# Switch experts' constants and first weights loaded in cross attention's projection; gather, both normalisations and transposes before retention in one block

## What is computed

```python
x = _layernorm(x + cross_attention(x, ctx))          # res @ Wproj + bproj at its end
# switch experts
logits = x @ Wr + br;  probs = softmax(logits)
gate = max(probs);  idx = argmax(probs);  mask = one_hot(idx, E)
pos = (cumsum(mask) * mask);  mask = mask * (pos < C)      # C = 100 slots of an expert
expert_in = einsum('nd,nec->ecd', x, dispatch)             # rows of x, times their gate
h  = relu(einsum('ecd,edf->ecf', expert_in, W1) + b1)
eo = einsum('ecf,efd->ecd', h, W2) + b2
x  = _layernorm(x + einsum('ecd,nec->nd', eo, combine))
# retention
xn = _ln(x, norm1_w, norm1_b)                              # a second normalisation of the same rows
q, k, v = xn @ wq + bq, xn @ wk + bk, xn @ wv + bv
...
x  = x + (silu(xn @ wg + bg) * groupnorm(retain(q, k, v))) @ wo + bo
```

## Time and profile before

| | us |
|---|---|
| median of 3 runs | 2859.72 |
| lowest, highest | 2859.01, 2860.47 |
| profiled execution, device time | 2862.07 |
| its span, from the first to the last instruction | 2860.3 |
| mean granted clock of TensorE, share of full speed | 0.938 |
| busy: TensorE, VectorE, ScalarE, GpSimd | 2507.9, 1402.8, 897.6, 557.9 |

### The profile page before, as it was taken

One profiled execution on the slowest core, in us unless ns is written; L12 is line 12 of the kernel. 1 busy time (PEld: TensorE's weight loads), 2 busy tenths in 40 slices (PEclk: granted clock), 3 DMA queues, 4 the chain that ended last, 5 costly groups with the idle time before them and its releaser, 6 DMA issues. The chain is left out here.

```text
span 2860.3 us, 32983 instructions
## 1 busy us (share of the span) xinstructions
PE 2507.9 (88%) x12313; PEld 1264.8 (44%) x12313; DVE 1402.8 (49%) x2005; ACT 897.6 (31%) x1869; POOL 557.9 (20%) x485
## 2 busy tenths in 40 slices
PE   7899999988999999896499899885997669999994
PEld 4544444434455555534245454353664323333331
DVE  5788888721578886721425512285444521111113
ACT  3644544402533334401112210085333112212210
POOL 0055555500000000001201100000000033343343
PEclk9899999999999999998799899997998879999997
DMA  2022222136535544308340000112000151560633
GB/s 86 25 72 82 75 85 79 66 87 241 187 112 185 175 139 120 126 15 243 117 156 0 2 39 3 50 41 88 1 1 1 53 233 52 232 265 23 261 101 116
DMA packets 94553, 288.64 MB, mean 101 GB/s; under 512 B 26924, under 2 KB 57288, under 8 KB 80188
## 3 DMA queue, kind: packets, MB, share of 16 engines
q1 hardware_dynamic: 59308, 158.34, 16.8%
q0 software_dynamic: 35104, 128.36, 12.6%
HBM read 449.40 MB, written 47.11 MB: 174 GB/s over the span
## 5 line engine op out<-in xcount | busy, mean ns | idle before, releaser
L684 POOL TENSOR_TENSOR x_rows<-ms_state,mb_C_everywhere 128x800 f32<-128x800 f32 x128 | 241.2, 1884 | 312.5 <-DVE ms_state L661 181.4
L694 PE MATMUL psum<-ms_context,mb_key_w 128*128 128x361 f32 x768 | 269.4, 487 | 23.0 <-ACT x_rows L604 9.6
L915 PE MATMUL psum<-at_Wv,at_context 128*128 128x512 f32 (+1 forms) x576 | 266.1, 601 | 0.0
L661 DVE TENSOR_TENSOR_SCAN ms_state<-ms_decay,psum 128x800 f32<-128x800 f32 x128 | 232.2, 1814 | 58.2 <-ACT ms_decay L611 41.3
L2639 PE MATMUL psum<-tf_W,tf_x_T 128*64 128x512 f32 x1024 | 232.3, 601 | 8.9 <-DMA tf_W<-in_L_W,tt_weight_row 8.9
L2661 PE MATMUL psum<-tf_W,tt_hidden 128*64 128x512 f32 x1024 | 227.2, 595 | 0.2 <-DMA tf_W<-in_L_W,tt_weight_row 0.2
L2694 ACT ACTIVATE tt_hidden<-psum,tf_b 128x64 f32<-128x64 f32 x512 | 111.7, 329 | 364.7 <-PE psum L2650 364.7
L694 PEld LDWEIGHTS psum<-ms_context,mb_key_w 128*128 128x128 f32 x768 | 136.3, 190 | 163.0 <-ACT x_rows L599 64.4
L2584 POOL DMA_INDIRECT tf_W<-in_L_W,tt_weight_row x128 | 126.9, 991 | 231.9 <-PE psum L2639 151.9
L1016 ACT ACTIVATE at_prob<-psum,at_neg_max 100x722 f32<-100x722 f32 x128 | 110.4, 863 | 145.9 <-DVE at_neg_max L1078 145.6
L1078 DVE TENSOR_REDUCE at_neg_max<-psum 100x1 f32<-100x722 f32 x128 | 115.6, 904 | 78.3 <-PE psum L936 77.9
(11 more groups left out here) (459 smaller groups left out, 3870.5 us busy)
## 6 DMA issues: line engine op xcount, KB each, us to landing
at_piece<-in_L_W_f POOLq DMA_DIRECT2D x24, 1024.0 KB, 6.3
keys_dram<-x_rows SPq DMA_DIRECT2D x128, 180.5 KB, 1.9
at_k_cols<-keys_dram SPq DMA_DIRECT2D x64, 361.0 KB, 3.2
sf_W<-in_L_W SPq DMA_DIRECT2D x16, 1024.0 KB, 7.5
tf_W<-in_L_W SPq DMA_DIRECT2D x8, 2048.0 KB, 26.0
ms_context<-in_ctxT SPq DMA_DIRECT2D x16, 541.5 KB, 4.4
at_context<-in_ctxT SPq DMA_DIRECT2D x8, 1083.0 KB, 5.1
ternary_dram<-at_piece_made POOLq DMA_DIRECT2D x14, 512.0 KB, 4.0
```

What stands on the lines that cost most here:

```text
L661: nc.vector.tensor_tensor_scan(state[:, n % RH, :], decay[:, g % RA, :, :].rearrange("p b l -> p (b l)"), drive[:, n % RD, :], 0.0, ALU.mu ...
L684: nc.gpsimd.tensor_tensor(seen[:, n % RH, :], state[:, n % RH, :], cC[:, n, :], ALU.mult).then_inc(weighed, 1)
L694: last = nc.tensor.matmul(side[:, 0:SH], lhsT=wk[:, k, e * P:(e + 1) * P], rhs=keys[:, h, k, :], start=(k == 0), stop=(k == KC - 1))
L915: last = nc.tensor.matmul(bank[0:rows_of(t), :], lhsT=ctxT[:, b % 2, k, t * P:t * P + rows_of(t)], rhs=wv[:, k, h * BANK:(h + 1) * BANK], ...
```

## The change

1. `project_norm` gets `early`, called on SP after the projection's own loads, and `keep`, by which SP stores each normalised sequence of x to DRAM as soon as it is ready, in 8 transfers of 200 KB. `switch_experts` now allocates its tiles first and passes in, as `early`, the loads of Wr and the five constants, of W1 and W2 of experts 0 and 1, and of b1 and b2. The loop of weight loads has one turn less. The release between the two blocks is gone.
2. The logits are made with x^T as stationary operand (100 columns) and Wr (8 columns) streaming, 4 matmuls a sequence, directly in the layout that was made by transposes; ScalarE's copies and the transposes are gone.
3. `gather_norm` and `normed_cols` in front of retention become one block, `gather_cols`. The second normalisation follows from the first's statistics: with v the variance, its rows are (x - mean) * (v (1 + eps) + eps^2)^-0.5. VectorE makes these, from the unscaled sum, and they are transposed. The rows of `c.x`, normalised once, are made by GpSimd, 8 `tensor_scalar` of 100x512, after VectorE's, and the block ends after them. There are two groups of 4 sequences. A release now stands between the experts and this block, and none inside it.
4. SP issues retention's loads of the vectors, wq, wk, bias rows, bo, decay, gn rows, wv, wg and wo at the start of `gather_cols`; their tiles are allocated there. The gathered rows use the space of w_in, which is loaded in the next block as before.

```diff
@@ project_norm, SP @@
+            if early is not None:
+                early(sp)
+            if keep is not None:
+                for b in range(NB):
+                    sp.wait_ge(normed, b + 1)
+                    sp.dma_start(keep[b * L:(b + 1) * L, :], c.x[:, b, :]).then_inc(kept, 16)
@@ switch_experts @@
+        def early(sp):
+            route.early(sp)
+            ffn.early(sp)
+
+        project(early, x_dram, x_stored)
+        block = ctx.enter_context(nc.Block())
@@ switch_route @@
-    def sync(sp):
+    def early(sp):
         sp.dma_start(wr[:, :, :], dram["L0_Wr"]).then_inc(wr_loaded, 16)
         for dst, src in consts:
             sp.dma_start(dst, src).then_inc(loaded, 16)
-        sp.dma_start(x_dram.rearrange("(b l) d -> l b d", l=L), c.x[:, :, :]).then_inc(x_stored, 16)
 
     def tensor(pe):
         pe.wait_ge(wr_loaded, 16)
-        for h in range(2):
+        for b in range(NB):
             for k in range(KD):
-                last = nc.tensor.matmul(c.banks[h][0:NE, 0:HALF], lhsT=wr[:, k, :], rhs=c.xT[:, k, h * HALF:(h + 1) * HALF],
+                last = nc.tensor.matmul(score[:, b, :], lhsT=c.xT[:, k, b * L:(b + 1) * L], rhs=wr[:, k, :],
                                         start=(k == 0), stop=(k == KD - 1))
-            last.then_inc(scored, 1)
-        for b in range(NB):
-            pe.wait_ge(score_cols, b // HB + 1)
-            last = nc.tensor.transpose(score[:, b, :], logit_cols[:, b * L:(b + 1) * L], c.ident[0:NE, 0:NE])
         last.then_inc(logits, 1)
     def scalar(act):
-        for h in range(2):
-            act.wait_ge(scored, h + 1)
-            nc.scalar.copy(logit_cols[:, h * HALF:(h + 1) * HALF], c.banks[h][0:NE, 0:HALF]).then_inc(score_cols, 1)
@@ switch_ffn @@
+    def early(sp):
+        for j in range(2):
+            for n, (w, name) in enumerate(((w1, "L0_W1"), (w2, "L0_W2"))):
+                sp.dma_start(w[j][:, :, :], dram[name][j]).then_inc(w_loaded[j][n], 16)
+        sp.dma_start(b1[:, :, :], dram["L0_b1"]).then_inc(b_loaded, 16)
+        sp.dma_start(b2[:, :, :], dram["L0_b2"].partition_broadcast(CAP)).then_inc(b_loaded, 16)
-        with sp.Fori(0, NE // 2) as i:
+        with sp.Fori(0, NE // 2 - 1) as i:
-                    sp.wait_ge(used, i * 2 + j + 1)
+                    sp.wait_ge(used, i * 2 + j + 3)
-        pool.wait_ge(x_stored, 16)
+        pool.wait_ge(x_stored, 16 * NB)
@@ retention @@
-        normed_cols(c, "re_norm1", c.x, vec, 0, dram["L1_vec"])
-        retain(c, vec, x1, [(w_in, "L1_w_in"), (b_in, "L1_b_in")])
+            gather_cols(c, gate, row, y_dram, vec, w_in, early)
+            retain(c, vec, x1, w, w_loaded, rows, rows_loaded, [(w_in, "L1_w_in"), (b_in, "L1_b_in")])
@@ gather_cols, new @@
+        @block.sync
+        def _(sp):
+            sp.dma_start(vec[:, :, :], dram["L1_vec"]).then_inc(vec_loaded, 16)
+            early(sp)
+
+        @block.gpsimd
+        def _(pool):
+            own = Chain(pool, chain_p)
+            for b in range(NB):
+                nc.gpsimd.indirect_dma_start(y[:, b, :], None, y_dram[:, :],
+                                             bass.IndirectOffsetOnAxis(ap=row[:, 0, b:b + 1], axis=0)).then_inc(y_loaded[b], 16)
+            own(nc.gpsimd.memset(power[:, :], -0.5))
+            for z, (lo, hi) in enumerate(groups):
+                pool.wait_ge(var_ready, hi)
+                own(nc.gpsimd.tensor_scalar(both[:, lo:hi], mv[:, lo:hi, 1], 1.0 + EPS, EPS * EPS, ALU.mult, ALU.add))
+                nc.gpsimd.tensor_tensor(both[:, lo:hi], both[:, lo:hi], power[:, lo:hi], ALU.pow).then_inc(both_ready, 1)
+            own(nc.gpsimd.tensor_scalar(rstd[:, :], mv[:, :, 1], EPS, None, ALU.add))
+            own(nc.gpsimd.tensor_tensor(rstd[:, :], rstd[:, :], power[:, :], ALU.pow))
+            pool.wait_ge(normed, NB)
+            for b in range(NB):
+                nc.gpsimd.tensor_scalar(c.x[:, b, :], c.x[:, b, :], mv[:, b, 0:1], rstd[:, b:b + 1], ALU.subtract, ALU.mult).then_inc(once, 1)
+            pool.wait_ge(once, NB)
```

More of the change, by code:

```diff
@@ L184, in bank_cols, with project_norm @@
     return bank[:, 0:KD * L].rearrange("p (k l) -> p k l", k=KD)
-def project_norm(c, name, KT, lhs, weight, weight_dram, residual, to_xT=True, store=False, part=None, bias=None, k_rows=P, more=None, x_dram=None, other=None):
+def project_norm(c, name, KT, lhs, weight, weight_dram, residual, to_xT=True, store=False, part=None, bias=None, k_rows=P, more=None, x_dram=None, other=None, early=None, keep=None, kept=None):
     nc = c.nc
@@ L757, in cross_attention @@
         attend(c, resT, projw, k_dram)
[L758 to L759 removed]
+        then(lambda early, keep, kept: project_norm(c, "xa_proj", KI, lambda k, b: resT[:, k, b * L:(b + 1) * L], projw, None,
+                     plus_rows(c), bias=dram["L0_bproj"], early=early, keep=keep, kept=kept))
 def attend(c, resT, projw, k_dram):
@@ L1252, in _, with switch_experts @@
                 norm.apply(nc, z, rows, c.x, normed)
[L1255 removed]
+def switch_experts(c, gate, row, y_dram, project):
     nc = c.nc
     x_dram = nc.dram_tensor("sw_x_dram", (T, D), F32, kind="Internal").ap()
[L1258 removed]
     with ExitStack() as ctx:
[L1260 to L1278, removed]
[L1280 to L1294 removed]
@@ new lines, in early, with _ @@
+        def early(sp):
[5 more added lines that the diff above has]
+        def _(sp):
+            ffn.sync(sp)
+        @block.gpsimd
+        def _(pool):
+            ffn.gpsimd(pool)
+        @block.tensor
+        def _(pe):
+            route.tensor(pe)
+            ffn.tensor(pe)
+        @block.scalar
+        def _(act):
+            route.scalar(act)
+            ffn.scalar(act)
@@ L1301, in switch_route, with _ @@
+        @block.vector
+        def _(dve):
+            route.vector(dve)
+            ffn.vector(dve)
+def switch_route(c, ctx, gate, row, table, slot_gate, table_ready):
     nc, dram = c.nc, c.dram
@@ L1517, with retention @@
 HID_LAST = HID - (KH - 1) * P
-def retention(c):
+def retention(c, gate, row, y_dram):
     nc, dram = c.nc, c.dram
@@ L1584, in _, with retain @@
                 last.then_inc(turned.done(b), 1)
-def retain(c, vec, x1, later):
+def retain(c, vec, x1, w, w_loaded, rows, rows_loaded, later):
     nc, dram = c.nc, c.dram
@@ L1594, in retain @@
         sem = lambda s: c.sem("rt_" + s)
-        w = {n: sb("w" + n, [P, KD, D]) for n in "qkvgo"}
-        w_loaded = {n: sem(f"w{n}_loaded") for n in "qkvgo"}
-        bias, bo, gn = sb("bias_rows", [L, 2, D]), sb("bo", [L, D]), sb("gn_rows", [L, 2, D])
-        decay, score = sb("decay", [L, KD, RG * L]), sb("score", [L, KD, RG * L])
+        bias, bo, gn, decay = rows
+        score = sb("score", [L, KD, RG * L])
         qT, kT = sb("q_cols", [P, KD, T]), sb("k_cols", [P, KD, T])
@@ L2731, in build @@
         c.release()
-        cross_attention(c, k_dram)
-        c.release()
-        for layer in (switch_experts, retention, ternary_attention, top2_experts):
+        y_dram = nc.dram_tensor("sw_y_dram", (NE * CAP, D), F32, kind="Internal").ap()
+        with ExitStack() as c2:
+            gate = c2.enter_context(nc.sbuf_tensor("sw_gate", [L, 1, NB], F32))
+            row = c2.enter_context(nc.sbuf_tensor("sw_row", [L, 1, NB], I32))
+            cross_attention(c, k_dram, lambda project: switch_experts(c, gate, row, y_dram, project))
+            c.release()
+            retention(c, gate, row, y_dram)
+            c.release()
+        for layer in (ternary_attention, top2_experts):
             layer(c)
```

112 lines of the change are left out of this document (81 added, 31 removed).

## The result

The changed kernel takes 2863.70 us (median of 20 runs, 2858.62 to 2870.75), the kernel before 2860.51 (20 runs, 2854.88 to 2865.58): a ratio of 1.0014, 95% interval 1.0008 to 1.0021. Forecast was 2842. The range was 2834 to 2853; the time lies far outside it, on the side of a little slower. The profiled execution after has a span of 2858.7 us and a time of 2860.79.

A forecast was written before the change was run, and what follows sets the result against it. It took the bound to vary by stage along one chain: waits for gathers, TensorE in the experts, VectorE and GpSimd before retention. Gains of 12.6 and 5.0 make 17.6 us, off the median 2859.72: 2842, range 2834 to 2853.

The forecast's parts named there:

- (f): End of the block before retention: no wait for wq, but eight GpSimd scalings of x at 1.0 us; +2.0 us won.
- rival D: GpSimd's scaling ends the block late: 3.3 us each eats the whole gain, 3.5 gives 2862 us; chance 0.03.
- (g): Gathers of y before retention contend with retention's loads issued at the block's start: 7.0 us lost, between 2 and 16.
- (a): Router logits: earlier start and narrow matmuls, 5.6 us at full clock or 11.0 at half; +4.0 us won.
- (d): Boundary between experts and the gather of y now holds the clearing of semaphores: 0.8 us lost.
- Rival B: Gathers of y wait as x's did, 16 us: gain 8.6, time 2851 us; chance 0.15.
- part 1: Switch layer (logits, gather of x, experts, boundary into gather of y): 12.6 us won, between 8.0 and 13.4.
- part 2: From the gather of y into retention: 5.0 us won, between -6 and +13.
- (b): Gather of x in the switch layer meets an empty queue, its loads moved into the projection: +9.4 us won.
- Rivals A: Gathers of y barely feel the loads, costing 2 us instead of 7: 2837 us; chance 0.15.
- E: Gathers of x are slow by themselves and the loads only fill the time: about 2860 us; chance 0.04.
- Rival C: Router logits run at the half clock: gain 13.0, time 2847 us; chance 0.10.

The follow-up runs named there:

- both repairs: Changed kernel, but VectorE scales x in retention's first loop instead of GpSimd, and SP issues retention's loads after all y gathers landed: 2835.09 us, ratio 0.9901.

## Why the prediction was wrong

**(f) is the term that failed, and its sign with it.** The working took 1.0 us for a GpSimd scaling, between 0.49 and 1.21, and I called 1.21 an upper bound because the new operation reads one tensor, not two. That reason was false: 2.07 was measured. With eight of them the tail is 16.5 + 0.7 (the first starts 0.7 us after VectorE's last scaling, when GpSimd's own second power is done) + 1.6 to the first matmul = 18.85, and not 8.6: 10.2 us. The price of a scaling makes 8.5 of them; 0.7 is the late start and 1.0 the end of the block, put at 0.6, which measures 1.6 behind GpSimd's scalings here and 0.8 behind VectorE's drains in the kernel with both repairs. "A GpSimd scaling over 2 us" stood among the signs of being wrong. The mechanism, a maximum of transposes and GpSimd, was right and was rival D's; D was put where a scaling takes 3.3 us and more (3.2 by its own terms, (17.6 + 8.0) / 8, since 0.6 of the 8.6 is no scaling), which holds only with every other term as forecast. With (g), (a) and (d) as measured 17.6 - 7.4 - 2.9 = 7.3 us are left, and a scaling of (7.3 + 8.0) / 8 = 1.9 us eats them. The bound from which D decides hangs on the other terms; I had reckoned it at their likeliest values alone.

**(g) had the right mechanism and half the size.** 14.35 us, near the bound of 16 taken from x's gathers. I took 7.0 for the first use (9.1 measured, the value in the earlier trace rows) and a pace of 2.1 us (2.8 measured), a pace lower than the 2.4 that x's rows showed, on the ground that small rows load in between. The rows of this kernel with gathers beside loads said 9 to 20 us each time; the choice in the middle had no row behind it. Rival B held that case: 7 us of the error. With (f) right and (g) as measured the kernel would have been at about 2842 + 7.4 = 2849, with (a) as measured too at 2852, still inside the range. The range itself was narrower than the bounds of the terms: part 1 at 8.0 and part 2 at -6 give 2858.

**(a) was right but for the clock.** The start held; the duration was 9.0, between the 5.6 and 11.0 of the two clocks. I reasoned that the matmuls begin at 2.4 GHz and that TensorE is then busy; it fell all the same, with TensorE at 1.00 busy. 2.6 us.

**(b), (c), (d) and (e) held** within 0.3 us: 9.3 for 9.4, 0 for 0, -1.1 for -0.8, 10.3 for 10.0. Loads moved into the projection cost TensorE nothing (58.68 us from its first matmul to the start of the last transposes, before and after), and the part with them is worth 10.6 us alone. Rivals A and E fall: the gathers of y felt the loads in full, those of x were slow only because of the loads beside them. Rival C's clock came true in part.

**The better version** is the change with both repairs: 2834.88 over nine runs on two chips, 0.990 to 0.991 of the kernel before, 25 to 27 us faster. Its two traces are 21.9 us shorter in the seam; both are of executions some 5 us above their medians (2840.05 and 2839.66).

## What to carry to other kernels

A load issued early is free only if nothing latency-bound shares the DMA engines: here the same move won 9.3 us where it took loads from in front of gathers, and lost 14.4 where it put them beside gathers; a wait on the engine that issues the loads gave those back. Before handing work to GpSimd as a side job, look for a row of that very form, with its number of arithmetic steps, and ask whether the end of a block waits for it; a row of another form with as many elements is no bound. When a sum rests on a maximum, work out the point where it turns with the other terms at their bad ends.

## What the runs showed of the hardware

- GpSimd, 100x512 in 4 bytes: subtract and multiply by values per row 2.07 us, one step with a constant 1.49, a sum of two tensors 1.26, a copy 0.61. VectorE does the first in 0.49.
- Gathers of 100 rows of 2 KB: landed 3.7 to 4.6 us after issue with no loads beside them, 10.6 to 19.5 beside 1 MB loads of 8 KB a partition, 9.5 to 12.3 beside loads in pieces of 2 KB.
- The granted clock fell to 0.50 under matmuls with 8 columns that followed one another without a gap (two traces); where they began at 0.50 (six) it did not return for their 10.8 us. Wide ones in the same place kept it at 1.00 (two traces), or had it back after 3 us (two) or 5.7 (one).
- Retention from wq to wo, all but the same work in thirteen traces, took 78.6 to 81.9 us, in step with the granted clock there (0.94 to 0.77 in its slowest 30 us): a difference of 2 us between two single traces can be this.
